# Cross-attention on one core: query block outermost, keys and values streamed per unit, scores as four row strips, projections in column strips beside every key tile

## The reference

```
ss = silu(c) @ W_ss + b_ss ; scale, bias = split(ss)        (once for x, once for ctx)
xq  = (1 + scale_q)  * layernorm(x)   + bias_q
xkv = (1 + scale_kv) * layernorm(ctx) + bias_kv
q = xq @ Wq + bq ;  k, v = split(xkv @ Wkv + bkv)           (16 heads of 32)
attn = softmax(q k^T / sqrt(32)) over the 3202 keys
return x + (attn v) @ Wp + bp
```

## Time and profile before

| what | value |
|---|---|
| median of 3 runs | 2373.68 us (2369.85 to 2376.54) |
| the profiled execution, first to last instruction | 2371.8 us |
| its own time with what lies around it | not listed apart; the median of the runs is 1.9 us above the span |
| PE busy | 2308.8 us |
| DVE busy | 1936.1 us |
| ACT busy | 1806.9 us |
| stages | prologue to 257.1, attention to 2329.2, end to 2371.8 us |

### The profile page before, as it was taken

How to read it: one execution, slowest core, us unless ns; L and a number is a source line. 1 busy time by engine, 2 the same in 40 slices (tenths; PEclk the granted TensorE clock), 3 DMA queues, 4 the chain that set the end, 5 groups by cost and what they waited for, 6 DMA issues and landing times.

```text
span 2371.8 us, 34855 instructions
## 1 busy us (share of the span) xinstructions
PE 2308.8 (97%) x12234; PEld 1028.5 (43%) x12234; DVE 1936.1 (82%) x1153; ACT 1806.9 (76%) x1822; POOL 62.2 (3%) x46
## 2 busy tenths in 40 slices
PE   7998799999999999999998999999999999999998
PEld 3456344444443444444443444444443334444343
DVE  4564588888889888888887888898888988888886
ACT  1333588888888888888887888888888977777772
POOL 1111000000001000000001000000001000000000
PEclk9999799999999999999999999999999999999999
DMA  6777911111117211111137111111154222332223
GB/s 231 265 267 259 185 54 54 54 53 53 52 27 147 65 54 54 54 44 54 53 72 158 54 54 35 35 47 53 53 114 92 68 60 67 95 94 78 72 60 127
DMA packets 135663, 211.65 MB, mean 89 GB/s; under 512 B 15016, under 2 KB 48296, under 8 KB 135532
## 3 DMA queue, kind: packets, MB, share of 16 engines
q1 hardware_dynamic: 124572, 186.70, 29.1%
q0 software_dynamic: 3376, 12.85, 1.7%
q10 hardware_dynamic: 7584, 10.49, 1.2%
HBM read 138.18 MB, written 71.82 MB: 89 GB/s over the span
## 4 chain that ended last, share of the span: by engine, by line
PE 85%; issue 1%; POOL 1%; ACT 1%; DVE 1%; DMA 0%; SPq 0%; ACTq 0%; POOLq 0%; DVEq 0%
PE ring L890 33%; PE o_ps L905 32%; PE l_ps L964 4%; PE l_ps L973 4%; PE l_ps L985 4%; PE l_ps L926 1%; POOL g_max L859 1%; PE ring L985 1%; PE o_ps L911 1%; PE l_ps L923 1%; PE ring L878 1%; ACT pt L1126 1%; DMA vg<-v_full 0%; DVE acc L1202 0%; DVE s_max L1213 0%
## 5 line engine op out<-in xcount | busy, mean ns | idle before, releaser
L1126 ACT ACTIVATE pt<-ring,shift 128x1024 f32<-128x1024 f32 x1600 | 1678.5, 1120 | 312.5 <-PE ring L890 296.4
L1202 DVE TENSOR_TENSOR acc<-acc,pt 128x2048 f32<-128x2048 f32 x672 | 1516.7, 2288 | 104.4 <-ACT pt L1126 104.0
L890 PE MATMUL ring<-qs,ks 128*128 128x512 f32 x3200 | 1005.2, 436 | 18.9 <-ACT pt L1126 18.9
L905 PE MATMUL o_ps<-pt,vg 128*32 128x512 f32 x6400 | 855.6, 607 | 0.0
L890 PEld LDWEIGHTS ring<-qs,ks 128*128 128x128 f32 x3200 | 563.2, 189 | 470.8 <-ACT pt L1126 306.2
L1202 DVE TENSOR_TENSOR acc<-pt 128x2048 f32<-128x2048 f32 x64 | 146.7, 2292 | 140.6 <-ACT pt L1126 140.6
L905 PEld LDWEIGHTS o_ps<-pt,vg 128*32 128x32 f32 x6400 | 126.2, 108 | 294.7 <-issue 225.7
L973 PEld LDWEIGHTS l_ps<-work 128*128 128x128 f32 x672 | 86.0, 190 | 121.6 <-issue 121.6
L964 PE MATMUL l_ps<-work 128*128 128x256 f32 x336 | 117.4, 431 | 0.0
L973 PE MATMUL l_ps<-work 128*128 128x128 f32 x672 | 114.0, 297 | 0.0
L331 PE MATMUL bank<-xt,wq 128*128 128x512 f32 x256 | 111.9, 595 | 0.0
(11 more groups left out here) (79 smaller groups left out, 670.1 us busy)
## 6 DMA issues: line engine op xcount, KB each, us to landing
qs<-q_split SPq DMA_DIRECT2D x128, 256.0 KB, 5.0
ks<-k_split SPq DMA_DIRECT2D x80, 320.0 KB, 6.6
work<-ctx_t SPq DMA_DIRECT2D x21, 1024.0 KB, 7.6
k_split<-work SPq DMA_DIRECT2D x42, 256.0 KB, 2.1
x_bias<-xb ACTq DMA_DIRECT2D x8, 1024.0 KB, 9.1
q_split<-hi SPq DMA_DIRECT2D x8, 1024.0 KB, 9.2
q_split<-lo SPq DMA_DIRECT2D x8, 1024.0 KB, 11.2
o_sums<-o_sb SPq DMA_DIRECT2D x32, 256.0 KB, 7.4
```

The source lines that it names most:

```text
L890: mm = nc.tensor.matmul(ring[:, bank + i, :], ks[:, h, t * P:(t + 1) * P], qs[U.par][:, h, :], start=True, stop=not exact)
L905: mm = nc.tensor.matmul(o_ps[cols, :], vg[:, t, cols], pt[t % PR][:, h, :], start=(t == 0), stop=False, skip_group_check=True)
L1126: nc.scalar.activation(pt[t % PR][:, 2 * pair:2 * pair + 2, :], ring[:, bank:bank + 2, :], ACT.Exp, scale=SCALE, bias=bias[:, :]).then_inc ...
L1202: nc.vector.tensor_tensor(a[:, :, :], (pt[t - 1] if k <= 2 else a)[:, :, :], pt[t % PR][:, :, :], ALU.add).then_inc(p_added, 1)
```

## The change

- **Loops.** The query block is the outer loop and the group the inner one: unit u is block u // 4, group u % 4. Keys (`ks`) and values (`vg`) of the next group are loaded for every unit, in five chunks, each behind the unit's own use of that chunk (`load_kv`).
- **Prologue.** The 7 ctx blocks and the first x block go through it, in the order of `SEQ`; each ctx block is projected to all keys and all values (512 features each), and stored to HBM. The other 7 x blocks are normalised, turned, modulated and projected beside the key tiles of the block before.
- **Scores.** No high and low parts: keys and queries are plain float32. A score matmul has the 32 features of its head as contraction, and the four heads of a tile lie in four row strips of the array, each with its own PSUM bank. There is one wait ahead of all four and one signal behind them: PE waits until the first exponential of the tile before is done, ACT waits for all four.
- **Banks.** The sums of P V change between banks 6 and 7 from unit to unit (`o_bank`); the other of the two takes the side work (`side_bank`), one job after the other in a fixed list. `free` waits until ACT has read the job before.
- **Side work** is cut into pieces of 32-column weights in four column strips. A later unit (g = 1 to 3) has 4 steps of 176 and 8 of 168 output columns, 2 of denominators and 8 of queries with 256 columns, and two halves of the tail's weighting (`weigh_tail`, 256 columns). A first unit (g = 0) has 8 query, 8 output, 2 denominator and 2 tail pieces of 256 columns, four steps of four transposes, and one step of the tail scores of all 16 heads with 512 columns. ACT reads each job out after the exponentials of the next step, with the functions shown.
- **Tails.** The two last keys of all 16 heads are scored and exponentiated once per block, not once per unit; their part of the denominators is added from HBM (`invert`).
- **DVE** gets, per block, the division (128x2048), the bias on the residual (128x2048), four residual additions of 512 columns, and the statistics and normalising of a later block of x.
- The residual is read from x itself; `x_bias` and `ctx_t` are no longer stored. The exact second version is rewritten in the same way.
- **End.** One block of outputs remains behind the last unit, with three of four groups done before the last denominators.

```diff
-    q_dram = nc.dram_tensor("q_split", [2, H, LQ], F32).ap()
-    k_dram = nc.dram_tensor("k_split", [2, H, KP], F32).ap()
-    v_dram = nc.dram_tensor("v_full", [KP, H], F32).ap()
-    xt_dram = nc.dram_tensor("ctx_t", [H, KP], F32).ap()
...
+    q_dram = nc.dram_tensor("q_full", [H, LQ], F32).ap()
+    k_dram = nc.dram_tensor("k_full", [H, LKV], F32).ap()
+    v_dram = nc.dram_tensor("v_full", [LKV, H], F32).ap()
+    pt_dram = nc.dram_tensor("p_tails", [NH * TAIL, LQ], F32).ap()
...
+            SEQ = [("c", 0), ("c", 1), ("x", 0)] + [("c", c) for c in range(2, KB)]
...
+            OUT_CUTS = (0, 176, 344, QB)
...
+            def o_bank(u):
+                return 6 + u % 2
+
+            def side_bank(u):
+                return 7 - u % 2
...
+                    def load_kv(u, c):
+
+                        if u > 0:
+                            sp.wait_ge(pv_done, NT * (u - 1) + CT * (c + 1))
+                        g = u % NG
+                        keys = slice(c * CT * P, (c + 1) * CT * P)
+                        sp.dma_start(ks[:, keys], k_dram[g * P:(g + 1) * P, keys]).then_inc(k_in[c], 16)
+                        sp.dma_start(vg[:, c * CT:(c + 1) * CT, :], v_dram[keys, g * P:(g + 1) * P]
+                                     .rearrange("(t p) n -> p t n", p=P)).then_inc(k_in[c], 16)
...
+                    for s in range(N_SEQ):
+                        kind, c = SEQ[s]
+                        for i in range(FT):
+                            keys_or_queries(s, i)
+                            if s == 1 and i == 0:
+                                modulation_columns(0, v_before(1) - 1)
+                            if kind == "c" and (c < KB - 1 or i < 2):
+                                values(s, i)
+                            if i == 1 and s + 1 < N_SEQ:
+                                if s == SAMPLE_AFTER + 1:
+                                    pe.wait_ge(sample_max, NG)
+                                transposes(s + 1)
...
+                    def scores(u, t):
+
+                        g = u % NG
...
+                        if t % CT == 0:
+                            pe.wait_ge(k_in[t // CT], 32 * (u + 1))
+                        if n > 0:
+                            pe.wait_ge(e_done, n - 1)
+                        for h in range(HG):
+                            i = n + h // 2
+                            mm = nc.tensor.matmul(bank[:, 2 * (i % RING) + h % 2, :], ks[rows_of(h), t * P:(t + 1) * P],
+                                                  qs[rows_of(h), g, :], start=True, stop=True)
+                        mm.then_inc(s_ready, 1)
...
+                    def weigh(u, t):
+
+                        pe.wait_ge(e_done, items(u) + 2 * t + 2)
...
+                        if t == 0 and u > 0:
+                            pe.wait_ge(job_taken, JOB["o", u - 1])
+                        for h in range(HG):
+                            mm = nc.tensor.matmul(bank[rows_of(h), o_bank(u), :], vg[:, t, rows_of(h)],
+                                                  pt[t % PR][:, h, :], start=(t == 0), stop=False, skip_group_check=True)
+                        mm.then_inc(pv_done, 1)
...
+                    def project_queries(u, b, m, half, k):
+                        job = ("q", b, m, half)
+                        if k == 0:
+                            free(job)
+                        for c in range(HG):
+                            col = m * P + c * DH
+                            mm = nc.tensor.matmul(bank[rows_of(c), side_bank(u), halves_of(half)], wq[:, k, col:col + DH],
+                                                  xt[:, k, halves_of(half)], start=(k == 0), stop=(k == FT - 1),
+                                                  skip_group_check=True)
+                        if k == FT - 1:
+                            mm.then_inc(job_done, 1)
...
+                        for c in range(HG):
+                            row = j * P + c * DH
+                            mm = nc.tensor.matmul(bank[rows_of(c), side_bank(u), cols], on[:, k, row:row + DH],
+                                                  wp[:, k, cols], start=(k == 0), stop=(k == NG - 1),
...
+                    def first_side(u, b, t):
+                        if b > 0:
+                            if t < 4:
+                                project_queries(u, b, 3, 0, t)
+                            if 4 <= t < 6:
+                                denominators(u, u - 1, t - 4)
+                            if 6 <= t < 10:
+                                project_queries(u, b, 3, 1, t - 6)
+                            if 16 <= t < 20:
+                                output(u, b - 1, 0, 0, t - 16)
+                            if 20 <= t < 24:
+                                output(u, b - 1, 0, 1, t - 20)
+                        if b + 1 < NB and t in (10, 12, 13, 14):
+                            turn_queries(u, b + 1, max(t - 11, 0))
+                        if t == 11:
+                            tail_scores(u, b)
+                        if t in (15, 24):
+                            weigh_tail(u, t // 24)
+
+                    def later_side(u, b, g, t):
+                        if b > 0:
+                            if t < 4:
+                                output(u, b - 1, g, 0, t)
+                            if 6 <= t < 10:
+                                output(u, b - 1, g, 1, t - 6)
+                            if 10 <= t < 14:
+                                output(u, b - 1, g, 2, t - 10)
+                        if 4 <= t < 6:
+                            denominators(u, u - 1, t - 4)
+                        if b + 1 < NB:
+                            if 14 <= t < 18:
+                                project_queries(u, b + 1, g - 1, 0, t - 14)
+                            if 18 <= t < 22:
+                                project_queries(u, b + 1, g - 1, 1, t - 18)
+                        if t in (22, 24):
+                            weigh_tail(u, t // 24)
...
+                    for u in range(UNITS):
+                        b, g = divmod(u, NG)
+                        for t in range(NT):
+                            if t + 1 < NT:
+                                scores(u, t + 1)
+                            elif u + 1 < UNITS:
+                                scores(u + 1, 0)
+                            weigh(u, t)
+                            if g == 0:
+                                first_side(u, b, t)
+                            else:
+                                later_side(u, b, g, t)
...
+                    pe.wait_ge(on_ready, last + 1)
+                    for j in range(2):
+                        last_output(j, range(NG - 1))
...
+                    for h in range(HG):
+                        nc.tensor.matmul(bank[rows_of(h), side_bank(UNITS), :], ones[:, :], acc[(UNITS - 1) % 2][:, h, :],
+                                         start=True, stop=False, skip_group_check=True)
+                    for h in range(HG):
+                        mm = nc.tensor.matmul(bank[rows_of(h), side_bank(UNITS), :], ones_blk[:, h, :], p_tail[:, :],
+                                              start=False, stop=True, skip_group_check=True)
+                    mm.then_inc(job_done, 1)
+                    for j in range(2, TPB):
+                        last_output(j, range(NG - 1))
+                    pe.wait_ge(on_ready, last + 2)
+                    for j in range(TPB):
+                        last_output(j, [NG - 1])
...
+                        for pair in range(2):
+                            n = items(u) + 2 * t + pair
+                            first = 2 * (n % RING)
+                            act.wait_ge(s_ready, NT * u + t + 1)
+                            nc.scalar.activation(pt[t % PR][:, 2 * pair:2 * pair + 2, :], bank[:, first:first + 2, :],
+                                                 ACT.Exp, scale=SCALE, bias=shift[:, g:g + 1]).then_inc(e_done, 1)
...
+                    for u in range(UNITS):
+                        b, g = divmod(u, NG)
+                        for t in range(NT):
+                            weights(u, t)
+                            if t == 0 and u > 0:
+                                take_sums(u - 1)
+                            if g == 0:
...
+                                if b > 0 and t == 6:
+                                    take_denominators(u, u - 1)
+                                if b > 0 and t == 10:
+                                    take_queries(u, b, 3, 1)
+                                if b + 1 < NB and t == 11:
+                                    modulate_queries(u, b + 1, 0)
+                                if t == 12:
+                                    take_tail(u, b)
+                                if b + 1 < NB and 13 <= t < 16:
+                                    modulate_queries(u, b + 1, t - 12)
+                                if b > 0 and t == 20:
```

(33 more changed lines are left out.)

2077 lines of the change are left out of this document (1056 added, 1021 removed).

## The result

After the change the kernel takes **2271.2 us** (median of four runs, 2269.04 to 2272.75), before it 2373.76 (four runs, 2369.85 to 2376.54). The ratio is 0.9567, with a 95% interval of 0.9553 to 0.958: faster by 4.3%. The forecast was 2267, range 2170 to 2420.

The account below looks back on a forecast made before the run. PE was taken to bound the kernel, through a key tile's cost and the PE-ACT ring. Prologue 240, units 1999 and end 26 gave a 2265 span; with 1.9 above it, 2267 us, range 2170 to 2420.

Parts of the forecast that it names:

- Scores, 1.08: Score phase of a key tile on PE: 0.11 first load, 0.87 four row strips, 0.10 shape change; 1.08 us, before 1.12.
- Rivals 1 to 3: Score phase: loads in series, 2531 (chance 0.15); strips pay in part, 2330 to 2430 (0.10); strips don't overlap, 4350 (0.03).
- Rival 4: Score phase: loads hide behind the weighting, scores 0.97, loop 2.25, time 2180; chance 0.10.
- The ring, 2.36: PE-ACT loop per tile without side work: exponential 1.12, signal 0.04, scores 1.16, signal 0.04; 2.36 us, before 2.12.
- A later unit, 61.9: Units g = 1 to 3: 12 steps of 2.51, 13 of 2.37, plus 1.0 for ACT's side work; 61.9 us.
- A first unit, 65.3: Units g = 0: 20 steps of 2.51, four of 2.68, one of 2.93, plus 1.5 for ACT's side work; 65.3 us.
- Blocks 0 and 7, -9: First block lacks outputs, last lacks queries: 0.14 less on some 40 steps and fewer modulations, 9 us less.
- VectorE covered by 4 us: DVE's work per unit, 57.7 us, fits under the later unit's 61.9; the division is ready about when first read.
- Rival 5: ACT's or DVE's in-order queue: a job not ready holds up exponentials 2 us a unit, +64, 2331; chance 0.05.
- DMA at nothing: Streamed keys and values, denominator stores and reciprocal loads during the units: issued early enough to cost nothing.
- Prologue, 240: Start to first exponential: projecting from near 24.5, ctx blocks of 30.1 each; 240 us, before 257.1.
- End, 26: After the last weighting: 12.4 with output matmuls covering DVE's last two additions, then 3.5 and 9.7; 26 us, before 42.6.

Follow-up runs that it names:

- e7: Kernel after the change, with the four heads' score matmuls sharing two row strips instead of four: 2973.03 us.
- e8: Kernel after the change, with keys and queries typed float32r so scores take one pass, less exact: 2066.99 us.
- e1: Kernel after the change, with one semaphore raised on ScalarE so the scores' wait stands on the exponential itself: 2238.03 us.
- e11: On top of e1, one semaphore raised on TensorE between the wait for keys and the wait for the exponential: 2229.08 us.
- e4: Kernel after the change, with one more 128x2048 VectorE addition per unit, at the unit's end: 2273.68 us.
- e6: Kernel after the change, with two more 128x2048 VectorE additions per unit, behind those of tiles 9 and 17: 2287.14 us.
- e3: Kernel after the change, with every chunk of values loaded a second time into unused space from the second unit on: 2273.18 us.
- e5: On top of e1, two semaphore instructions between the scores' wait and each tile's first exponential, one carrying that wait: 2312.95 us.
- e10: e8 together with the semaphore of e1: 2064.05 us.
- e2: Kernel after the change, with query and output side pieces as one 128-column matmul instead of four 32-column ones: 2339.92 us.

## Why the prediction was right, and where it was not

The mechanism was right: the four strips pay in full, the tile gets cheaper for TensorE, and the ring between TensorE and ScalarE gives part of it back. The time came out 4 us above the forecast, but that is luck in part, since the terms were off by up to 9 each way: prologue 8.4 too long, units 8.8 too short, end 1.9 too short.

- **Scores, 1.08:** measured 1.07. That is 0.2 over a single matmul; how much of it is the first load and how much the change of shape, no run separates. e7 shows that it is the four strips that make it so. Rivals 1 to 3 fall: the eight loads take 0.31 together, not 0.88, and the strips pay in full. The Trainium skill's 3.07 times for four row tiles ("TensorE: Matmul & The Clock Gate", "Part 3: Packing small matmuls") would give 1.24 a tile by the estimate made from it, 0.17 more than was measured. Rival 4 would have needed 0.97. Two figures beside the rivals were off. Rival 1's threshold of 0.04 for the spacing of the loads does not go with its own 1.41, where the eighth load ends the chain: 0.13 more needs some 0.085. And VectorE's 57.7 a unit was no bar: e8 has 56.
- **A step with a 256-column piece, 2.51:** measured 2.50. With transposes 2.68 was forecast and 2.65 measured, with tail scores 2.93 and 2.93.
- **The ring, 2.36:** this is the step that failed. The loop had 0.04 from the scores to ACT, taken from the earlier trace rows, where one wait stands on the instruction that needs it. With three waits the late one goes onto an instruction in front, and the bare step is 2.46. e1 takes that away and finds 2.376.
- **A later unit, 61.9:** measured 62.4. Its 13 steps without a 256-column piece took 0.09 more each, 1.2 in all; of the 1.0 set aside for ScalarE's side work 0.4 was there, and that turned out to be the steps at a new chunk of keys (e11).
- **A first unit, 65.3:** measured 63.8. The sum of its steps on TensorE, 63.8, was right; the 1.5 on top for modulations, sums and denominators was not there, since the steps with transposes took 2.65, which is TensorE's own. The two errors cancel, which is luck: a block of 251.0 was forecast, and blocks 1 to 6 took 250.8 to 251.8.
- **Blocks 0 and 7, -9:** here the units' 9 us are missing (1999 forecast, 2007.8 measured). I took 0.14 off each of the 40 steps that lose their 256-column piece there, and 3.4 for modulations. With the ring at 2.46 such a step is only 0.04 shorter than one of 2.50, and the modulations cost nothing to begin with: block 0 took 249.8 and block 7, to the end of its last exponential, 248.9, together 3.3 less than two of 251.0. That is 5.7 more than forecast; some 4 of it are the ring's error once more, and the rest is the modulations. The other 3 of the 9 lie in blocks 1 to 6 and behind the last exponential.
- **VectorE covered by 4 us:** 57.0 us of 62.7 a unit, so 5.7 by the sum, and e4 bears it out for one addition. At one place there was no cover to begin with: the division at tile 17 of a block's first unit, whose reciprocals come back by DMA only just in time. Rival 5 was a wait of this kind. In the kernel after it occurred clearly once, in block 4: VectorE waited 2.6 us for the reciprocals, and the step took 3.52 in place of 2.50 (0.8 of it as TensorE's wait for the division). In e6 it occurred in all seven.
- **DMA at nothing:** right for the keys and values, as e3 bears out. The loads of the reciprocals, which I had given time enough, are the exception just named.
- **Prologue, 240:** measured 231.6. Projecting starts at 23.9 (24.5 forecast). A context block takes 29.2 (116.5 to 145.7 on TensorE), not 30.1: I took 0.874 for a matmul by the length of its record, and matmuls in a row follow at 0.858; transposes take 1.75, not 2.1. That is 5 of the 8 us.
- **End, 26:** measured 27.9. The six output matmuls were to cover two additions of VectorE; from the last weighing there are three (2238.48 to 2245.29), and the denominators wait 0.7 for them. The last matmul of the range test then waits another 1.3 for VectorE.

## What to carry to other kernels

Look at which instruction a wait stands on: when an instruction needs several semaphores, put the ones that are long satisfied on an instruction in front and leave the late one on the instruction that starts the work. In this ring between two engines the wrong order costs 0.08 to 0.09 us per turn, together 42 us in 2271. Small matmuls beside others belong in the shape that their neighbour already has. And cover is to be checked where a result is read, not only by the sum of a unit: VectorE had 2.4 us a unit to spare when one step of a block had become 1.3 us longer by waiting for its division, and it stood idle, waiting for a DMA, just before that division.

## What the runs showed that I had not expected

- A semaphore instruction whose record is 38 ns long on ScalarE (51 on TensorE) costs 70 to 90 ns of a ring, on either engine (e1, e5, e11), and nothing clear of the intervals where the ring isn't the bound (e10).
- A full-array piece of 256 columns costs 0.084 more before row-strip scores than four column-strip pieces of the same columns do, over and above the 0.113 for the change of shape (e2). The cause of it was not tried.
- The scores in one pass take a unit from 62.7 to 56 us, with VectorE the next bound (e8).
